# A decoder layer on one core: row statistics and magnitudes folded into additions, the input norm moved to ScalarE

## What is computed

```python
def _layernorm(x, axis=-1, eps=1e-05):
    m = jnp.mean(x, axis=axis, keepdims=True)
    v = jnp.var(x, axis=axis, keepdims=True)
    return (x - m) / jnp.sqrt(v + eps)

x = x + attn(_layernorm(x))             # 16 heads of 32, linear attention with a causal mask,
                                        # q and k through two small maps each, head outputs root-mean-square normed, then @ wo.T
x = x + mixer(ctx_1024, _layernorm(x))  # input projection, 4-tap convolution, silu, a scan over positions with
                                        # 16 states per channel, and y * silu(z) with z the normed x
x = x + ffn(_layernorm(x))              # gate and value, 2048 hidden, weights ternary, and before each product:
    gamma_x = jnp.clip(jnp.max(jnp.abs(x), axis=-1, keepdims=True), 1e-05, None)
    scale_x = 127.0 / gamma_x
    x_dq = jnp.clip(jnp.round(x * scale_x), -128.0, 127.0) / scale_x
```

## Time and profile before

| | us |
|---|---|
| median of 3 runs | 931.2 |
| lowest and highest | 930.08, 934.58 |
| the profiled execution's own time | 933.21 |
| its span, first to last instruction | 931.4 |
| busy in the span: TensorE, VectorE, ScalarE, GpSimd | 791.9, 780.5, 584.6, 489.2 |

### The profile page before, as it was taken

How to read it: one execution, slowest core, us unless ns; L and a number is a source line. 1 busy time by engine, 2 the same in 40 slices (tenths; PEclk the granted TensorE clock), 3 DMA queues, 4 the chain that set the end, 5 groups by cost and what they waited for, 6 DMA issues and landing times. The chain is left out here.

```text
span 931.4 us, 11695 instructions
## 1 busy us (share of the span) xinstructions
PE 791.9 (85%) x4070; PEld 429.4 (46%) x4070; DVE 780.5 (84%) x913; ACT 584.6 (63%) x868; POOL 489.2 (53%) x292
## 2 busy tenths in 40 slices
PE   5859898369887888998978987998889899999798
PEld 1334555143452334665443333656445335664343
DVE  5887788996998986989699988589788998988875
ACT  3788899965647866445365866453455796453552
POOL 0456678786646523575447643276444755565020
PEclk8889997679789999989999999989998999999999
DMA  8687788866546535666534563456643565666000
GB/s 291 252 247 224 229 251 225 238 187 165 122 96 133 114 69 113 143 144 169 125 68 113 121 140 68 111 130 149 158 98 79 123 126 130 151 144 135 1 12 34
DMA packets 50781, 131.12 MB, mean 141 GB/s; under 512 B 7298, under 2 KB 7874, under 8 KB 50724
## 3 DMA queue, kind: packets, MB, share of 16 engines
q0 software_dynamic: 16128, 58.73, 33.4%
q1 hardware_dynamic: 34596, 71.65, 23.8%
HBM read 67.09 MB, written 4.35 MB: 77 GB/s over the span
## 5 line engine op out<-in xcount | busy, mean ns | idle before, releaser
L1730 POOL TENSOR_TENSOR W<-W,CROW 128x1024 f32<-128x1024 f32 x128 | 321.9, 2531 | 160.1 <-DVE W L1904 132.6
L1904 DVE TENSOR_TENSOR_SCAN W<-DEC,PB 128x1024 f32<-128x1024 f32 x125 | 285.1, 2281 | 10.2 <-ACT DEC L1353 4.0
L1743 POOL DMA_DIRECT2D ACC<-W x112 | 98.3, 878 | 155.1 <-DMA ACC<-W 132.0
L1893 DVE TENSOR_TENSOR PB<-DU,PB 128x1024 f32<-128x1024 f32 x128 | 156.5, 1223 | 13.7 <-PE PB L1060 10.1
L1353 ACT ACTIVATE DEC<-DT,ACOL 128x511 f32<-128x511 f32 x250 | 160.1, 710 | 11.5 <-DVE W L1904 11.4
L1116 PE MATMUL bank<-W,ARENA 128*128 128x512 fp8e4 x512 | 124.0, 386 | 0.0
L1308 ACT ACTIVATE ARENA<-bank 128x512 f32<-128x512 f32 x56 | 32.5, 592 | 73.4 <-PE bank L876 36.4
L1116 PEld LDWEIGHTS bank<-W,ARENA 128*128 128x128 bf16 x512 | 45.3, 98 | 61.2 <-issue 16.9
L1451 ACT ACTIVATE ARENA<-bank,SDQ 128x512 f32<-128x512 f32 x64 | 43.4, 685 | 46.0 <-PE bank L1116 45.8
L1060 PE MATMUL PB<-BC,ID 96*128 96x512 bf16 x98 | 39.3, 415 | 33.7 <-DVE W L1904 32.4
L876 PE MATMUL bank<-XNT,WK 128*128 128x512 f32 x128 | 63.7, 644 | 2.2 <-DVE ARENA L1936 2.2
(11 more groups left out here) (175 smaller groups left out, 1333.2 us busy)
## 6 DMA issues: line engine op xcount, KB each, us to landing
ACC<-W POOLq DMA_DIRECT2D x112, 512.0 KB, 4.6
CROW<-c_rows SPq DMA_DIRECT2D x98, 256.0 KB, 3.6
W<-in_wffn SPq DMA_DIRECT2D x27, 512.0 KB, 6.2
X<-in_wffn SPq DMA_DIRECT2D x21, 512.0 KB, 5.8
X<-in_x SPq DMA_DIRECT2D x7, 1024.0 KB, 8.6
out_dram<-X SPq DMA_DIRECT2D x16, 256.0 KB, 2.2
X<-in_ctxT SPq DMA_DIRECT2D x4, 512.0 KB, 5.6
ARENA<-in_x SPq DMA_DIRECT2D x1, 1024.0 KB, 5.6
```

The costliest lines, as they stand in the source:

```text
L1730: pool.tensor_tensor(w, w, CROW[k % 2][:, :].unsqueeze(1).broadcast_to([P, 2, L]), ALU.mult)\
L1743: pool.dma_start(ACC[accumulator(u)][:, :, :], w, accum_op=ALU.add).then_inc(y_summed, 16)
L1893: dve.tensor_tensor(into, du, rows, ALU.mult).then_inc(dbu_done.sem, 1)
L1904: dve.tensor_tensor_scan(flat(W[u % 4]), flat(decay_of(u)), flat(PB[:, scan_bank(u):scan_bank(u) + 2, :]), 0.0, ALU.mult, ALU.add).then_in ...
```

## The change

Four edits, all of them in how the norms are made; the tables of points are as they were.

- The input's norm goes from VectorE to ScalarE. VectorE makes a shift XSHIFT = -mean * rstd for the four tiles (`norm_shift`), in `attention` ahead of `feature(b, g, 1)` at the last group, in the first row where `normed` stood. ScalarE's new `normed` computes x * rstd + XSHIFT in four activations, in `attention` between `square(b, g - 1)` and the point ("a", g, 1), in the first row right after `rstd(0, 0)`.
- The statistics ahead of the gate go. `residual` becomes an addition that also sums its result over the row (TOTALS); `mixer_mean` scales that to -mean (NMEAN), one column per tile; ScalarE's `deviations` squares x - mean and sums (VAR, the squares themselves go to Z and are overwritten by the gate), four activations ahead of `rstd(f, 1)`, whose logarithm now scales by 1/D.
- `add_mixer` also takes the row's least value (LOW).
- The norm ahead of the feed-forward also takes the largest normed value (HIGH); the least one follows from LOW (DEEP = (mean - LOW) * rstd), and the magnitude is the larger of the two. The reduction of OT goes.

```diff
+            def deviations(f, t):
+                act.wait_ge(*mean_ready.at(f, t + 1))
+                act.activation(Z[:, t, :], X1[:, t, :], ACT.Square, bias=NMEAN[:, t:t + 1],
+                               accum_out=VAR[:, t:t + 1]).then_inc(var_ready.sem, 1)
+
             def rstd(b, i):
-                act.wait_ge(*ln_stats[i].at(b))
-                act.activation(LNV[i > 0][:, :], MV[i > 0][:, :, 1], ACT.Ln, bias=EPSC[:, :]).then_inc(ln_log[i].sem, 1)
+                if i == 1:
+                    act.wait_ge(*var_ready.at(b))
+                    act.activation(LNV[1][:, :], VAR[:, :], ACT.Ln, bias=EPSC[:, :], scale=1.0 / D)\
+                       .then_inc(ln_log[i].sem, 1)
...
+            def normed(b):
+                act.wait_ge(*xshift_ready.at(b))
+                for t in range(TT):
+                    act.activation(XROWS[b][:, t, :], XROWS[b][:, t, :], ACT.Identity, bias=XSHIFT[:, t:t + 1],
+                                   scale=RSTD[0][:, t:t + 1]).then_inc(xn_ready.sem, 1)
...
                     if g > first_group(b):
                         square(b, g - 1)
+                    if b + 1 < BATCH and g == GROUPS - 1:
+                        normed(b + 1)
                     decays(b, "a", g, 1)
...
                 rstd(0, 0)
+                normed(0)
                 act.wait_ge(setup_v, SETUP_V - 2)
                 decay(0)
...
+                for t in range(TT):
+                    deviations(f, t)
                 rstd(f, 1)
...
-            def normed(b, i, src, ready):
-                dve.wait_ge(*ln_rstd[i].at(b))
-                dst = src if i == 0 else OT
+            def norm_shift(b):
+                dve.wait_ge(*ln_rstd[0].at(b))
+                dve.scalar_tensor_tensor(XSHIFT[:, :], MV[0][:, :, 0], -1.0, RSTD[0][:, :], ALU.mult, ALU.mult)\
+                   .then_inc(xshift_ready.sem, 1)
+
+            def normed_peak(f, t):
+                dve.tensor_tensor_reduce(OT[:, t, :], X2[:, t, :], MV[1][:, t, 0:1].broadcast_to([P, D]),
+                                         RSTD[1][:, t:t + 1], -LARGEST, ALU.subtract, ALU.max, HIGH[:, t:t + 1])\
+                   .then_inc(xn2_ready.sem, 1)
+
+            def normed_peaks(f):
+                dve.wait_ge(*ln_rstd[2].at(f))
+                dve.tensor_tensor(DEEP[:, :], MV[1][:, :, 0], LOW[:, :], ALU.subtract).then_inc(deep_step.sem, 1)
                 for t in range(TT):
-                    dve.tensor_scalar(dst[:, t, :], src[:, t, :], MV[i > 0][:, t, 0:1], RSTD[i > 0][:, t:t + 1],
-                                      ALU.subtract, ALU.mult).then_inc(ready.sem, 1)
+                    if t == 1:
+                        dve.wait_ge(*deep_step.at(f, 1))
+                        dve.tensor_tensor(DEEP[:, :], DEEP[:, :], RSTD[1][:, :], ALU.mult).then_inc(deep_step.sem, 1)
+                    normed_peak(f, t)
...
             def row_scales(f):
                 dve.wait_ge(*xn2_ready.at(f))
-                dve.tensor_reduce(AMX[:, :], OT[:, :, :], AX.X, ALU.max, apply_absolute_value=True)\
-                   .then_inc(q_step.sem, 1)
+                dve.wait_ge(*deep_step.at(f))
+                dve.tensor_tensor(AMX[:, :], DEEP[:, :], HIGH[:, :], ALU.max).then_inc(q_step.sem, 1)
...
             def residual(f, t):
...
-                dve.tensor_tensor(X1[:, t, :], R.bank(f, "wo", t)[:, :], X1[:, t, :], ALU.add)\
+                dve.tensor_tensor_reduce(X1[:, t, :], R.bank(f, "wo", t)[:, :], X1[:, t, :], 1.0, 0.0,
+                                         ALU.add, ALU.add, TOTALS[:, t:t + 1])\
                    .then_inc(R.drained(f, "wo", t), 1)
...
             def add_mixer(f, t):
                 dve.wait_ge(*R.full_at(f, "yT", t))
-                dve.tensor_tensor(X2[:, t, :], R.bank(f, "yT", t)[:, :], X1[:, t, :], ALU.add)\
+                dve.tensor_tensor_reduce(X2[:, t, :], R.bank(f, "yT", t)[:, :], X1[:, t, :], 1.0, LARGEST,
+                                         ALU.add, ALU.min, LOW[:, t:t + 1])\
                    .then_inc(R.drained(f, "yT", t), 1)
...
-            def mixer_sums(f, t):
+            def mixer_mean(f, t):
                 dve.wait_ge(*R.drained_at(f, "wo", t))
-                sums(f, 1, X1, t)
+                dve.tensor_scalar(NMEAN[:, t:t + 1], TOTALS[:, t:t + 1], -1.0 / D, None, ALU.mult)\
+                   .then_inc(mean_ready.sem, 1)
...
                     units(b, "a", g, 0)
+                    if b + 1 < BATCH and g == GROUPS - 1:
+                        norm_shift(b + 1)
                     feature(b, g, 1)
                     units(b, "a", g, 1)
-                    if b + 1 < BATCH and g == GROUPS - 1:
-                        normed(b + 1, 0, XROWS[b + 1], xn_ready)
```

More of the change, by code:

```diff
@@ L42 @@
 MAGIC = 12582912.0
+LARGEST = 3.4028234663852886e38
 UNITS = 2 * N
@@ L643, in decoder_layer @@
         NMR = sb("NMR", [P, TT])
+        XSHIFT = sb("XSHIFT", [P, TT])
+        TOTALS = sb("TOTALS", [P, TT])
+        NMEAN = sb("NMEAN", [P, TT])
+        VAR = sb("VAR", [P, TT])
         AMX = sb("AMX", [P, TT])
+        LOW = sb("LOW", [P, TT])
+        HIGH = sb("HIGH", [P, TT])
+        DEEP = sb("DEEP", [P, TT])
         AMC = sb("AMC", [P, TT])
@@ L713, in decoder_layer @@
         xn2_ready = signal("xn2_ready", TT)
+        deep_step = signal("deep_step", 2)
         q_step = signal("q_step", 5)
@@ L1680, in last_row @@
                 for pair in range(2):
+                    for t in (2 * pair, 2 * pair + 1):
+                        deviations(f, t)
                     rstd_tiles(f, 1, 2 * pair, 2 * pair + 2)
```

47 lines of the change are left out of this document (30 added, 17 removed).

## The result

The changed kernel takes 944.7 us (median of 6 runs, 940.25 to 951.38) against 931.3 of the kernel before beside it: a ratio of 1.0141, with a 95% interval of 1.0108 to 1.0174. It is slower by 13 us, where I forecast 932.1 and a range of 920 to 940. The profiled execution took 944.19 us with a span of 942.4; TensorE's mean granted clock is 0.919 of full speed, before 0.930. Every ratio and interval here leaves out runs that were more than 1.5% above the fastest of the same kernel, while every median is over all runs.

A forecast was written before the change was run, and what follows sets the result against it. TensorE (85% busy) and VectorE (84%) share the bound, neither saturated. The terms 2.5 + 0.2 + 1.7 - 1.5 - 0.1 - 0.6 - 1.5 + 0.2 sum to +0.9 us on 931.2, so 932.1, range 920 to 940.

The forecast's parts named there:

- place 1: First batch row's input norm: ScalarE's norms stand ahead of its copies, so the query projection starts later, +2.5 us.
- place 3: Third row's input: ScalarE's norms delay the transposed keys' drain and TensorE's key-value product, +1.7 us.
- Rival C: Row-wise results on VectorE run at the scan's slow rate, 1.14 us per norm with maximum: 938.7 us, chance 0.07.
- Place 2: Second row's input: ScalarE's new norms and wait fill its idle time, so VectorE's saving is not collected, +0.2 us.
- Place 4: Fourth row's input: TensorE's product moves later but the transposes behind it end earlier, -1.5 us.
- Rival B: The new four-column shift is held by GpSimd at places 2, 3 and 4: 937.5 us, chance 0.14.
- Places 5 and 6: Statistics after the attention (-0.1 and -0.6 us) and norm ahead of the feed-forward (-1.5 us), three rows each.
- Place 7: Last row: mean, square and read replace statistics and aggregation, with small changes on four later tiles, +0.2 us.
- Rival A: The relief arrives, ScalarE's added work lying in idle time except at place 1: 915.8 us, half 924, chance 0.27.

The follow-up runs named there:

- the kernel with this place alone: Kernel before with only the first row's input normed by ScalarE, shift computed column by column: 937.4 us, ratio 1.0049.
- the shift by columns: Changed kernel with the input norm's shift as four one-column VectorE operations with per-row scalars instead of one four-column operation: 937.3 us, ratio 1.0056.
- The foldings alone: Changed kernel with all four rows' inputs normed by VectorE as before, keeping only the folded totals and magnitudes: 934.0 us, ratio 1.0013.

## Why the prediction was wrong, point by point

In short, three terms of the sum failed. TensorE's clock stood at nothing in it, and cost 2.7 us at place 1 and 2.3 at place 3. The shift stood at 0.1 to 0.2 us in my forecast, and took 1.87 on average and up to 3.87. And the relief was placed where ScalarE is idle and not where its queue gets to the norms. Places 1 to 4 were to cost 2.9 us and cost 12.9.

- **Prices of the instructions: right.** Row-wise results cost 0.68 to 0.74 us with 0.08 for the read, ScalarE's norms 0.73 (2.93 for four). Rival C is refuted. The Trainium skill's rule on two fp32 SBUF sources and accumulator readback ("Vector Engine (DVE) Microarchitecture Reference", Points that are easy to get wrong) was weighed for the norm with a maximum. The trace shows nothing of it for this operation, which took 741 ns where the plain norm takes 661, and had its readback.
- **Place 1, +2.5: the walk was right, and the sum short by a term.** ScalarE's copies ended at 43.0 instead of 42.4, since it waited 0.98 us for the shift. The projection started at 43.25 instead of 39.90, 3.35 us late, and at 42.34 in the kernel with this place alone. The step that failed is "Nothing later in the first row hides it": I looked for what hides the cost and not for what enlarges it. The clock stood at 0.50 over the projection, +2.7 us, which makes 6.1 at the fourth scan. The waits in front of it had grown from 0.91 and 1.28 us to 2.20 and 1.56; that they brought the low clock is likely but not shown. From 26 to 52 us the clock averages 0.93 in the kernel before, 0.67 to 0.80 in the seven kernels with this row's norms on ScalarE, and 0.80 to 0.93 in the others. Alone the place cost 5.8 us by the medians and 4.6 by the ratio.
- **Place 2, +0.2: mis-sized, +2.5.** That is just outside my upper bound of 2.2. The balance of 4.1 us of new work against 3.97 us of idle time held: with an unheld shift the place stands at -0.2 up to the scan at 204.5. The step that failed is the wait for the shift, put at 1.2 us. ScalarE waited 2.96 us for it in the changed kernel, where the shift took 2.25 (the row stands below the table). And my walk ended at the copies of 193.43: behind them the unheld kernel loses 2.6 us as well, at the scan behind the transfer of weights. Norms behind the keys' drain gained 1.8 to 3.7 us up to 204.5, and 0.9 to 2.3 over the whole place.
- **Place 3, +1.7: the walk was right to 0.1 us.** I had the product at 428.35; the changed kernel runs 8.43 us late there (429.57 against 421.14 for the head's square), and 436.87 less 8.43 is 428.44. Missing again is the clock: the product took 2.93 us instead of 1.50 and the fillers 2.74 instead of 1.89, 2.3 us. The shift here ran nearly free (0.47 us) in the profiled execution; where it was held 2.6 to 2.7 us, in two other kernels, the place cost 6.3 and 6.5.
- **Place 4, -1.5: wrong sign, +1.3.** Rival B hit hardest here, 3.87 us, and on VectorE's own next step (the second feature, for which TensorE waited 3.19 us) and not on ScalarE's wait. With the shift by columns the place gave -2.1: the relief was there, within my bounds of -4.7 and -0.3. I had not seen that the kernel before already paid for a low clock at this place, which is why a handover without the wait is worth 6.0 us, more than my lower bound.
- **Rival B, +5.4 at a chance of 0.14: right in kind, and under-priced.** I had the held row of the gate's shift before me and set against it one row that was not held. With GpSimd at work half of the time, a chance nearer one half for each shift was at hand; of nineteen in the traces fourteen took over 0.5 us. I put each hold at 2.0 us, and it lasted to the end of three products in a row. The shift by columns gave back 7.4 us. The Trainium skill ("SBUF — State Buffer", Who interferes with whom) says that the later one of the two fully blocks. The traces agree in that the shift stands still, 3.87 us for 4 columns. They agree only in part in who is the later one: of the three GpSimd products the second and the third began after the shift had, and the shift went on waiting.
- **Places 5 and 6, -0.7 and -1.5: not to be told from nothing.** The foldings alone are 934.0 against 932.6, and singly 931.9 and 932.0 against 932.0 and 930.9. The squares went onto ScalarE just where VectorE then waits for it: before the gate's shift VectorE idled 6.1 us in three rows, 1.8 in the kernel before.
- **Place 7, +0.2: as forecast, as far as it was read** (the change is 10.9 us late at the last scan and 11.0 at the end; the rest of the last row was not read apart).
- **What is left.** The rest of the profiled execution, places 5 to 7 and all between, gained 2.0 us, and my places 5 to 7 add up to -2.0. Since the foldings alone gain nothing that can be measured, I count this as luck.
- **Rival A and the range.** ScalarE's added work was not in idle time, although idle time was there: it lay behind the keys' drain, and the change puts the norms ahead of that. My range went to 940 and took in B or the upper bounds, one at a time; B, the clock and the queue came together.

## What to carry to other kernels

Work moved to an engine with free time costs by its position in that engine's in-order queue: put it behind the drains that release the bound engine and ahead of the idle time, not at the point where its input happens to be ready (5.5 us here by the medians, 4.9 against the kernel before in each group). A four-column VectorE operation with two inputs in memory took 0.16 to 5.25 us here, by whether GpSimd was at work when it came; the form with per-row scalars, one column at a time, was never held. And when a step makes TensorE wait for some microseconds, read the granted clock in the windows behind that wait, in the kernel before as well: at place 1 the wait was a little over half of the cost, at place 4 a little under half of the gain.

## What the runs showed of the hardware

- A four-column operation of VectorE with two inputs in memory took 0.16 to 5.25 us, and 17 of 19 ended within 0.03 us of the end of a GpSimd product, the longest behind three in a row; one-column operations with per-row scalars took 0.19 to 0.21 us each, inside GpSimd's products too.
- The granted clock stood at 0.50 for some 10 us in the first row of the changed kernel (38.5 to 48.8 us), where TensorE had idled 2.20 us before it fell, and eight products of 512 columns took 6.41 us instead of 3.67. In other kernels the low stretch came earlier, once even over dense filler work. Where it falls differs between kernels with the same code up to that point; what decides this stays open.
- A row-wise result on the addition costs nothing over the plain addition at 512 elements (0.69 us both) but the read of 0.08 us; the norm with a maximum took 0.74 us where the plain one takes 0.66, and the read of 0.08.
